# A six-layer model on one core: a join without its barrier, token outputs kept partition by partition, and the shift of some transposed logits added by VectorE

## The reference, cut to what matters

```python
x = x + 0.5 * _L0_ffn_ref(_layernorm(x), ...)    # routed layer
x = x + _L0_attn_ref(_layernorm(x), ...)         # state space layer (mamba)
x = x + 0.5 * _L0_ffn_ref(_layernorm(x), ...)    # routed layer, the same weights
x = x + 0.5 * _L1_ffn_ref(_layernorm(x), ...)    # soft layer
x = x + _L1_attn_ref(_layernorm(x), ...)         # gated linear attention
x = x + 0.5 * _L1_ffn_ref(_layernorm(x), ...)    # soft layer, the same weights
```

```python
logits = (jnp.einsum('tzd,ed->tze', x, phi_w) + phi_b).reshape(t, z, n, p)   # n = 64 experts, p = 32 slots
D = jax.nn.softmax(logits, axis=3)
C = jax.nn.softmax(logits, axis=2)
X_tilde = jnp.einsum('tznp,tzd->npd', D, x)
...
Y = jnp.einsum('tznp,npH->tzH', C, Y_tilde)
```

## Time and profile before

| | us |
|---|---|
| median of 3 runs | 2271.38 |
| lowest and highest | 2268.46, 2273.17 |
| the profiled execution in all | 2270.07 |
| its span (first to last instruction) | 2268.3 |
| TensorE busy | 1895.5 (84%) |
| VectorE busy | 1579.1 (70%) |
| ScalarE busy | 1176.3 (52%) |
| GpSimd busy | 1230.6 (54%) |

### The profile page before, as it was taken

How to read it: one execution, slowest core, us unless ns; L and a number is a source line. 1 busy time by engine, 2 the same in 40 slices (tenths; PEclk the granted TensorE clock), 3 DMA queues, 4 the chain that set the end, 5 groups by cost and what they waited for, 6 DMA issues and landing times.

```text
span 2268.3 us, 24123 instructions
## 1 busy us (share of the span) xinstructions
PE 1895.5 (84%) x6160; PEld 920.9 (41%) x6160; DVE 1579.1 (70%) x2028; ACT 1176.3 (52%) x2808; POOL 1230.6 (54%) x796
## 2 busy tenths in 40 slices
PE   4099686888888724977999899998987999999998
PEld 3067532333333512754333344443343333344443
DVE  5223488999999831328999857664797999955544
ACT  2322186555555341216999753432446999854332
POOL 3735208999999564543999700000885999800000
PEclk9999898999999956988999999999899999999999
DMA  7123293544545121334000000000741200000000
GB/s 259 50 84 103 91 153 114 180 170 176 176 169 177 54 62 54 106 100 129 0 0 0 0 1 0 0 0 14 194 136 29 65 0 0 0 1 10 5 9 14
DMA packets 108463, 163.63 MB, mean 72 GB/s; under 512 B 11008, under 2 KB 74035, under 8 KB 108257
## 3 DMA queue, kind: packets, MB, share of 16 engines
q1 hardware_dynamic: 100194, 146.41, 21.7%
q0 software_dynamic: 8192, 16.30, 2.0%
HBM read 125.09 MB, written 38.14 MB: 72 GB/s over the span
## 4 chain that ended last, share of the span: by engine, by line
PE 42%; DVE 24%; issue 15%; POOL 10%; ACT 3%; DMA 2%; SPq 1%; DVEq 1%; POOLq 1%; another core or an unknown queue 0%; ACTq 0%; PEldq 0%
PE ps L1938 10%; PE ps L1911 10%; PE ps L1660 5%; DVE arena L1406 5%; PE ps L1670 5%; DVE arena L1412 4%; DVE arena L1404 4%; PE ps L1787 3%; PE ps L1912 2%; POOL arena L547 2%; DVE arena L1351 2%; POOL arena L610 2%; POOL arena L572 1%; DVE XN L1314 1%; POOL arena L616 1%
## 5 line engine op out<-in xcount | busy, mean ns | idle before, releaser
L1911 PE MATMUL ps<-XT,c_phiT 128*128 (+1 forms) x512 | 263.0, 595 | 3.9 <-DVE arena L1444 3.9
L1862 PE MATMUL ps<-arena 128*128 128x512 f32 x512 | 250.7, 612 | 16.3 <-POOL arena L572 16.2
L580 POOL TENSOR_TENSOR arena<-arena 128x864 f32<-128x864 f32 x128 | 210.1, 1642 | 84.6 <-DVE arena L1404 81.8
L1853 PE MATMUL ps<-c_phiT,arena 128*128 128x512 f32 x512 | 244.7, 601 | 5.4 <-DVE arena L1406 2.3
L572 POOL TENSOR_TENSOR arena<-arena 128x1024 f32<-128x1024 f32 x128 | 246.6, 1928 | 0.0
L1938 PE MATMUL ps<-arena 128*128 128x512 f32 x512 | 227.6, 603 | 11.1 <-DVE arena L1472 11.1
L610 POOL TENSOR_TENSOR arena<-arena 128x1024 f32<-128x1024 f32 x32 | 63.7, 2000 | 305.1 <-DMA arena<-value_rows 305.0
L1472 DVE TENSOR_TENSOR arena<-arena 128x4096 f32<-128x4096 f32 x32 | 140.2, 4422 | 120.5 <-ACT arena L905 120.5
L898 ACT ACTIVATE arena<-ps 128x512 f32<-128x512 f32 x256 | 151.1, 597 | 106.4 <-PE ps L1912 106.1
L515 POOL DMA_INDIRECT token_outputs<-arena x128 | 124.3, 971 | 149.4 <-DVE arena L1252 115.8
L849 ACT ACTIVATE arena<-arena 128x32 f32<-128x32 f32 x640 | 195.8, 311 | 0.0
(11 more groups left out here) (235 smaller groups left out, 3612.3 us busy)
## 6 DMA issues: line engine op xcount, KB each, us to landing
arena<-input_gates SPq DMA_DIRECT2D x128, 512.0 KB, 3.7
arena<-value_rows SPq DMA_DIRECT2D x32, 512.0 KB, 5.1
arena<-slot_inputs SPq DMA_DIRECT2D x32, 258.0 KB
arena<-in_L_ffn_w SPq DMA_DIRECT2D x32, 256.0 KB
arena<-token_outputs SPq DMA_DIRECT2D x16, 512.0 KB, 7.0
slot_inputs<-arena SPq DMA_DIRECT2D x1, 4128.0 KB, 13.4
slot_inputs<-zero SPq DMA_DIRECT2D x1, 4128.0 KB, 33.2
token_outputs<-arena SPq DMA_DIRECT2D x1, 4096.0 KB
```

What stands on the lines that cost most here:

```text
L580: pool.tensor_tensor(Ed[:, r, PSLOT * NA:].rearrange("p (n q) -> p n q", q=PSLOT), Lc[:, r, PSLOT * NA:].rearrange("p (n q) -> p n q", q=P ...
L1853: ins = pe.matmul(pbank(2 * h + c), xts[:, r // 2, :], phiT[:, at:at + CHUNK], start=True, stop=True)
L1862: ins = pe.matmul(pbank(4 + 2 * h + c), xns[:, r // 2, :], Dd[:, r, CHUNK * c:CHUNK * (c + 1)], start=start, stop=stop, skip_group_check=True)
L1911: pe.matmul(pbank(t % 4), phiT[:, P * t:P * (t + 1)], xt(b, c), start=True, stop=False)
```

## The change

In words it was described as: the same join, but the last two chunks of the routed layers stored by whole chunks of 512 rows, not tile by tile. The diff has no edit of the storing loop (`store`, L511). What it has:

- The token outputs are kept by partition: `ytok` is read as "(p t q) d" instead of "(t p q) d", and the constant `k_row_id`, from which the rows of the scatter follow, is numbered to match. A partition's two rows for the four tiles of one gather now lie in one piece of 4 KB.
- The barrier behind the first routed layer is gone (`stage_end` only for m = 1, the count lowered by one). In its place SyncE's clearing DMAs wait for the eighth addition of the join (`gated`), GpSimd's memset for the eighth sum (`y_sum`). The first half batch's u is projected behind the sixth transposition of the join (`project_u`), copied behind the last `ln_scale` (`copy_u`), and its first taps stand ahead of the last `ln_copies`. The transpositions use bank 4 in both routed layers. The padding is cleared ahead of the join.
- In the loops of the soft layers the tiles from 11 (s = 0) or 9 (s = 1) to 15 get no L1912 matmul. One such matmul per chunk goes to bank 4, ScalarE copies it to `mS` at tile 6, VectorE adds it to each of these tiles from PSUM into `Ec` (`less_m`), and ScalarE's exponential reads `Ec` in place. `less_m` stands ahead of `ln_apply` and `normalise` on VectorE. Some semaphores are merged: `Z` and `bank4`, `Rz` and `token_rows`, `g_diff` and `gates`.

```diff
+BY_PE = (11, 9)
...
-            eng.wait_ge(sem("stage"), ENGINES * k)
+            eng.wait_ge(sem("stage"), ENGINES * (k - 1))
...
-                yv = ytok[m].rearrange("(t p q) d -> p t q d", p=P, q=K)
+                yv = ytok[m].rearrange("(p t q) d -> p t q d", p=P, q=K)
...
-                stage_end(sp_, k + 1)
+                if m == 1:
+                    stage_end(sp_, k + 1)
...
+            sp_.wait_ge(sem("gated"), CHUNKS)
             clear(disp[1], "disp_zero")
             clear(ytok[1], "ytok_zero")
...
+            pool.wait_ge(sem("y_sum"), CHUNKS)
             pool.memset(dts[:, :, :], 0.0).then_inc(sem("ones"), 1)
...
                 for c in range(CHUNKS):
                     ln_scale(n, c)
+                    if c == CHUNKS - 1 and m == 0:
+                        copy_u(0, 0, 0, True)
                     if c:
-                        ln_copies(n, (c - 1) // 2, (c - 1) % 2, 0)
-                ln_copies(n, BATCH - 1, 1, 0)
-                stage_end(act, k + 1)
+                        ln_copies(n, (c - 1) // 2, (c - 1) % 2, 4)
+                if m == 0:
+                    act.wait_ge(sem("prepared"), U_PADDED)
+                    first_taps(0, 0)
+                ln_copies(n, BATCH - 1, 1, 4)
+                if m == 1:
+                    stage_end(act, k + 1)
...
-                        act.activation(Ec[c][:, t, :], pbank(t % 4), ACT.Exp)\
-                            .then_inc(sem("Ec"), 1)
+                        if not first and t == 6:
+                            hold(act, sem("bank4"), sums_count(s, v) - 1)
+                            act.activation(mS, pbank(4), ACT.Copy).then_inc(sem("token_rows"), 1)
+                        logit = pbank(t % 4)
+                        if not first and t >= BY_PE[s]:
+                            hold(act, sem("less_m"), less_m_count(s, v, t))
+                            logit = Ec[c][:, t, :]
+                        act.activation(Ec[c][:, t, :], logit, ACT.Exp).then_inc(sem("Ec"), 1)
...
+                if m == 0:
+                    chain(dve.memset(u_pad[:, :, 0:CONV_PAD], 0.0))
+                    dve.nop().then_inc(sem("prepared"), 1)
                 for grp in range(TILES // GROUP):
...
+                def less_m(v, c):
+                    dve.wait_ge(sem("token_rows"), sums_count(s, v) - 1)
+                    dve.wait_ge(sem("yT_ps"), v - 1)
+                    for t in range(BY_PE[s], ST):
+                        dve.wait_ge(sem("LT"), ST * v + t + 1)
+                        dve.tensor_tensor(Ec[c][:, t, :], pbank(t % 4), mS, ALU.add).then_inc(sem("less_m"), 1)
+
...
                 with dve.Fori(1, CHUNKS // 2) as i:
+                    less_m(base + 2 * i, 0)
                     if s == 0:
                         ln_apply(4, 2 * i - 2, 0)
                     normalise(base + 2 * i, 0)
                     residual(base + 2 * i - 1, i - 1, 1)
+                    less_m(base + 2 * i + 1, 1)
...
                     if c + 2 < CHUNKS:
                         weigh(c + 2)
-                    ln_turn(2 * m + 1, c, c % 2, 0)
-                stage_end(pe, k + 1)
+                    ln_turn(2 * m + 1, c, c % 2, 4)
+                    if c == 5 and m == 0:
+                        pe.wait_ge(sem("ln_XT"), CHUNKS + 1)
+                        project_u(0, 0, 0)
+                if m == 1:
+                    stage_end(pe, k + 1)
...
-                    for d in range(DT):
-                        if not (first and h == 0):
-                            pe.wait_ge(sem("u_sb"), DT * (v - 1) + d + 1)
-                        pe.matmul(pbank(d), W_in[:, P * d:P * (d + 1)], xt(b, h), start=True, stop=True).then_inc(sem("u_ps"), 1)
+                    if first and h == 0:
+                        pe.wait_ge(sem("gated"), CHUNKS)
+                    else:
+                        if first:
+                            pe.wait_ge(sem("ln_XT"), 2 * CHUNKS)
+                        project_u(v, b, h)
...
-                        pe.matmul(pbank(t % 4), phiT[:, P * t:P * (t + 1)], xt(b, c), start=True, stop=False)
-                        pe.matmul(pbank(t % 4), row128[:, :],
-                                  mCT[:, ds(b * TIME + CHUNK * c, CHUNK)], start=False, stop=True).then_inc(sem("LT"), 1)
+                        m = mCT[:, ds(b * TIME + CHUNK * c, CHUNK)]
+                        if loop and t == 4:
+                            pe.wait_ge(sem("lnz"), v)
+                            pe.matmul(pbank(4), row128[:, :], m, start=True, stop=True).then_inc(sem("bank4"), 1)
+                        without_m = loop and t >= BY_PE[s]
+                        ins = pe.matmul(pbank(t % 4), phiT[:, P * t:P * (t + 1)], xt(b, c), start=True, stop=without_m)
+                        if not without_m:
+                            ins = pe.matmul(pbank(t % 4), row128[:, :], m, start=False, stop=True)
+                        ins.then_inc(sem("LT"), 1)
...
-        "k_row_id": (K * np.arange(TOKENS).reshape(TILES, P).T + 1).astype(f),
+        "k_row_id": (K * np.arange(TOKENS).reshape(P, TILES) + 1).astype(f),
```

More of the change, by code:

```diff
@@ L671, in _, with copy_u, first_taps @@
             ln_copies(0, BATCH - 1, 1, 0)
+            def copy_u(v, b, h, first):
+                for d in range(DT):
+                    hold(act, sem("u_ps"), DT * v + d + 1)
+                    if h == 0 and not first:
+                        hold(act, sem(f"conv{d}"), v)
+                    act.activation(u_pad[:, d, CONV_PAD + CHUNK * h:CONV_PAD + CHUNK * (h + 1)], pbank(d), ACT.Copy)\
+                        .then_inc(sem("u_sb"), 1)
+            def first_taps(v, h):
+                for d in range(DT):
+                    hold(act, sem("u_sb"), DT * v + d + 1)
+                    if not below(v, 1):
+                        hold(act, sem("uc"), DT * (v - 1) + d + 1)
+                    act.activation(cacc[:, d, :], tap(d, h, 0), ACT.Copy, scale=conv_w[:, d, 0:1]).then_inc(sem(f"tap{d}"), 1)
             def experts(m, k):
-                hold(act, sem("g_diff"), m + 1)
+                hold(act, sem("gates"), 2 * m + 1)
                 act.activation(g1[5], g1[4], ACT.Exp).then_inc(sem("g_exp"), 1)
@@ L725, in project @@
                     v = 2 * b + h
-                    for d in range(DT):
-                        hold(act, sem("u_ps"), DT * v + d + 1)
-                        if h == 0 and not first:
-                            hold(act, sem(f"conv{d}"), v)
-                        act.activation(u_pad[:, d, CONV_PAD + CHUNK * h:CONV_PAD + CHUNK * (h + 1)], pbank(d), ACT.Copy)\
-                            .then_inc(sem("u_sb"), 1)
-                    for d in range(DT):
-                        hold(act, sem("u_sb"), DT * v + d + 1)
-                        if not below(v, 1):
-                            hold(act, sem("uc"), DT * (v - 1) + d + 1)
-                        act.activation(cacc[:, d, :], tap(d, h, 0), ACT.Copy, scale=conv_w[:, d, 0:1]).then_inc(sem(f"tap{d}"), 1)
+                    if not (first and h == 0):
+                        copy_u(v, b, h, first)
+                        first_taps(v, h)
                     for d in range(DT):
@@ L1285, in experts @@
                 ln_apply(2 * m + 1, CHUNKS - 1, 1)
-                stage_end(dve, k + 1)
+                if m == 1:
+                    stage_end(dve, k + 1)
             experts(0, 0)
-            chain(dve.memset(u_pad[:, :, 0:CONV_PAD], 0.0))
-            dve.nop().then_inc(sem("prepared"), 1)
             def split_bc(v, b, h):
@@ L1640, in xt, with project_u @@
                 return XT[:, ds(b, 1), CONV_PAD + CHUNK * h - shift:CONV_PAD + CHUNK * (h + 1) - shift].rearrange("p a t -> p (a t)")
+            def project_u(v, b, h):
+                for d in range(DT):
+                    if not below(v, 1):
+                        pe.wait_ge(sem("u_sb"), DT * (v - 1) + d + 1)
+                    pe.matmul(pbank(d), W_in[:, P * d:P * (d + 1)], xt(b, h), start=True, stop=True).then_inc(sem("u_ps"), 1)
             def experts(m, k):
@@ L1929, in total @@
                     pe.wait_ge(sem("tree"), 5 * (v + 1))
-                    pe.matmul(pbank(4), same_p[:, :], t1, start=True, stop=True).then_inc(sem("Z"), 1)
+                    pe.matmul(pbank(4), same_p[:, :], t1, start=True, stop=True).then_inc(sem("bank4"), 1)
                 def combine(v, c, early):
@@ L1961, in soft @@
                         v = base + 2 * i + c
[L1962 removed]
+                        logits_T(v, i, c, False, loop=True)
                         combine(v - 1, 1 - c, False)
```

23 lines of the change are left out of this document (13 added, 10 removed).

## The result

The changed kernel took 2254.12 us in the median of 4 runs (2252.52 to 2257.64), the kernel before 2270.78 beside it: ratio 0.9929, 95% interval 0.9911 to 0.9946, or 16.7 us less. The profiled execution took 2252.52 us in all with a span of 2250.7, which is 17.6 us less than the span before.

The account below looks back on a forecast made before the run. It took TensorE, busy without a break, to bound the soft layers' loops, and a chain of waits the join. Gains of 12.9 + 5.5 + 0 = 18.4 us gave 2251.7 us profiled, 2252.3 median; range 2247 to 2260.

Parts of the forecast that it names:

- the saved matmuls: Soft layers' loops: 4 and 6 fewer shift matmuls per chunk at 0.215 us, 5.2 and 7.7 us, together 12.9 us.
- The thin cover ahead of tile 15: First soft layer: tile 11's exponential ends at +15.0, TensorE wants its bank for tile 15 at +15.5; 0.5 us spare.
- Rival A: First soft layer: late VectorE or dear handoffs stall TensorE ahead of tile 15, its 5.2 us gone: 2257.5; chance 0.13.
- the first add therefore runs +13.6: First soft layer's chunk: VectorE free at +13.55, tile 11 ready at +13.05, so its add runs +13.6 to +14.3.
- VectorE as the bound (C): Soft loops: adds over 1.4 us make VectorE the bound, gain gone at 1.65 us; 2296 at 2.0 us; chance 0.05.
- The join, 5.5 us: After the first routed layer: without the barrier, the next taps start 5.5 us earlier, ends 5.0 and 5.7.
- GpSimd's 3.5 us memset moves from 282.99 to about 277 and its next work is far later: Join after the first routed layer: the earlier memset was listed among what is hidden, at no cost.
- That the scans start at least 5 us earlier: Stage after the join: scans starting less than 5 us earlier would show the forecast wrong.
- B: Join's gain given back in the projection's steady part, by DMA traffic of clears or stores, say: 2258; chance 0.10.
- the prediction's own signs of being wrong: TensorE gaps inside the loop, second taps not 5 us earlier, or next stage's scans less than 5 us earlier.
- The layout, 0: Gathers of token outputs in 4 KB pieces: no gain or loss; ends 0.5 us gained per gather or 1.2 us lost.
- D: Gathers: pieces at 32 KB pitch read at half rate, 1.2 us lost in each routed layer: 2254.7; chance 0.08.

Follow-up runs that it names:

- The kernel from tile 10: Changed kernel with tile 10's shift also given to VectorE in the first soft layer (6 tiles instead of 5): 2242.70 us, ratio 0.9945 to the kernel before.
- doubled adds: Changed kernel with every VectorE add of the loops done twice, the first into a free buffer: 2262.66 us, ratio 0.9946 to the kernel before.
- the join alone: Changed kernel with the soft layers' loops as before, so only join and layout changed: 2269.57 us, ratio 0.9999 to the kernel before.

## Why the prediction was right, and where it was not

The forecast was 2251.7 us for the profiled execution and 2252.3 for the median; they came to 2252.5 and 2254.1. (By its own addition, 1.3 us above the profiled execution, the median's figure should have been 2253.0.) The large term, the saved matmuls, came as forecast and for the reason given. That the sum is as near as 0.8 us is partly luck: the loops and the lead at the first scan make 15.5 us of the 17.6, and the other 2.1 come from stages for which the forecast had nothing.

- **TensorE's saved matmuls, 12.9 us: 12.6.** 4.84 of 5.2 and 7.76 of 7.7 us. Adds of 0.69 us for the 0.68 of the earlier trace rows. The figures of the model for tile times and for where VectorE comes free (+10.4, +13.55) were met to 0.1 us.
- **The thin cover ahead of tile 15, 0.5 us.** Rival A, in small: a stall of 0.16 to 0.19 us in two of the six chunks, those that follow a turn of the loop. The step "the first add therefore runs +13.6" left out the turn of the loop, 0.4 us on VectorE's queue. The kernel from tile 10 shows what a missing cover costs, 0.64 to 0.86 us a chunk. It was not "a microsecond late", so the 5.2 us of the first soft layer stayed but for 0.3.
- **VectorE as the bound (C).** Out: the column sum waits for TensorE, 3.2 to 3.6 us behind the tree for the 3.3 of the model and 4.1 for its 3.9, and doubled adds leave 12 us of gain. At 1.2 us an add neither the 1.4 us at which the tree would bind nor the break-even of 1.65 us was reached, and I measured no dearer one.
- **The join, 5.5 us: 3.6 at the second round of taps.** This is the term that was mis-sized. The step that failed is "GpSimd's 3.5 us memset moves from 282.99 to about 277 and its next work is far later". It looked for who waits for the memset, and not for what runs beside it: VectorE's placing, held for 3.3 us. With the memset elsewhere or gone the stage gives 5.4 to 6.1 us in four profiles (join 39.52, 39.12, 39.04 and 38.75 us), the size that was forecast.
- **What became of it later.** That the scans start at least 5 us earlier failed too: the first scan starts at 367.62 instead of 370.51, 2.9 us, since 0.7 more went between the last taps and the scan. That is B's outcome in small, but no run shows B's cause, the DMA traffic. Among the kernels with 128 rows the stage took 34.8 to 36.8 us (35.9 before), and the three shortest (34.8, 35.4 and 35.4) are those whose clock stayed at 1.00 in the first 10 us behind the last taps, where the others show 0.66 to 0.71 in the second 5 us. In the total the join alone shows 0 to 4 us. So of the prediction's own signs of being wrong two came clearly, 3.6 and 2.9 us where it wanted 5, and the third, a gap of TensorE inside the loop, as 0.19 us.
- **The layout, 0: 0.2 us for the first landing** in the two profiles, 0.14 on average over all, within the ends; D is out. By an estimate from the 207 GB/s of the Trainium skill, page "DMA: Bandwidth & Descriptors", section "Latency and other measured facts", which it measured at a pitch of 512 KiB, the landing would have been 1.2 us later. The traces go the other way at a pitch of 32 KB. The row that the 0 was taken from was a poor stand-in: the 512 KB reads of `input_gates` fetch one row of 4 KB for all 128 partitions, so they have no pitch.
- **What I had at no price**: the second join, 1.5 us shorter. That made up most of what the first lacked, so the sum came out nearer than its terms. It followed the time at which TensorE's clock rose there, and in three of ten profiles with this layout it did not come, so it is luck for the forecast.

## What to carry to other kernels

When a wait is taken away and an engine's work moves earlier, list what runs beside it at the new time on the engines that aren't waiting for it, not only who waits for its result. A cover of half a microsecond in a loop must be counted with the turn of the loop in it. And a term worth 3 us is better read from its own stage than from the medians of two totals, with the granted clock of that stage beside it: the same join took 41.3 to 44.3 us by what the clock did.

## What the runs showed of the hardware

- A GpSimd memset of 128x4096 float32 (3.55 us) held one of VectorE's tensor_scalar of 128x128 from SBUF to SBUF for 3.6 us instead of 0.3, and so the addition queued behind it; both ended within 0.1 us of the memset. So it was in all eight profiles in which the two met. Six scalar_tensor_tensor of 128x512 beside the same memset took their usual 4.06 us.
- TensorE at the step size matmuls kept to a granted clock of 0.50 (1.2 GHz) over 20 us in both kernels that contracted 25 rows, and stood between 0.66 and 1.00 in the twelve profiles with 128, zeros among them. Fewer rows made no matmul shorter (0.61 for 0.60 us at the higher level, 1.06 us at the lower with either), and this stage took 3.3 and 4.5 us more than in the change.
- After an idle time of 3.7 us TensorE went on at full clock (1.00) in three profiles with this join, and with stretches at 0.50 in four others.
- GpSimd's first drain behind a batch of its scatters to HBM ended 7.3 us after its last work in all 14 profiles, even where a memset or other work had come between; its other drains ended 0.05 to 0.08 us after it. In one kernel the slow one was the last to arrive at a barrier and cost 1.2 us.
- Gathers of 512 KB in pieces of 4 KB at a pitch of 32 KB ran at 410 to 421 GB/s, the same bytes in pieces of 1 KB at 380 to 385.
